# Layer 0's values: two halves of the array, or four quarters

## The reference, cut to what matters

```python
attn = jnp.einsum('bqhd,bkhd->hbqk', qh, kh)
attn = attn * mask[None]
attn = attn - jnp.max(attn)
attn = jnp.exp(attn) * mask[None]
attn = attn / (jnp.sum(attn, axis=-1, keepdims=True) + 1e-15)
out = jnp.einsum('hbqk,bkhd->bqhd', attn, vh).reshape(Bn, Tq, H * DK)
```

## Time and profile before

| | |
|---|---|
| three runs, median | 914.35 us |
| the profiled execution | 909.97 us |
| its span, first to last instruction | 908.2 us |
| PE busy | 861.4 us (95%), 4511 matmul records |
| DVE, ACT, POOL busy | 553.0, 416.2, 456.1 us |
| mean granted TensorE clock | 0.981 of full speed |
| L476, layer 0's values | 256 records, 62.0 us |
| L464, sums of both layers | 512 records, 68.2 us |
| first values step to the end of the loop | about 93 to 357 us |

### The profile page before, as it was taken

One profiled execution on the slowest core, in us unless ns is written; L12 is line 12 of the kernel. 1 busy time (PEld: TensorE's weight loads), 2 busy tenths in 40 slices (PEclk: granted clock), 3 DMA queues, 4 the chain that ended last, 5 costly groups with the idle time before them and its releaser, 6 DMA issues.

```text
span 908.2 us, 11986 instructions
## 1 busy us (share of the span) xinstructions
PE 861.4 (95%) x4511; PEld 577.5 (64%) x4511; DVE 553.0 (61%) x1050; ACT 416.2 (46%) x560; POOL 456.1 (50%) x284
## 2 busy tenths in 40 slices
PE   7989999999999989989989999999999999999865
PEld 6567475665747464467577587576775875767624
DVE  1347565656657575877575656655756566556646
ACT  2325363645545354633543644535536345353440
POOL 0520404124040424327689588687795886863714
PEclk9999999999999999998999999999999999999968
DMA  9613335161514225973531432424314334210011
GB/s 349 247 62 136 124 121 200 47 245 51 197 70 177 108 94 214 290 265 95 131 101 47 140 93 93 140 70 137 119 47 139 93 93 139 70 70 1 1 47 47
DMA packets 47641, 111.55 MB, mean 123 GB/s; under 512 B 4704, under 2 KB 8544, under 8 KB 47584
## 3 DMA queue, kind: packets, MB, share of 16 engines
q1 hardware_dynamic: 47584, 110.78, 36.4%
HBM read 76.69 MB, written 34.08 MB: 122 GB/s over the span
## 4 chain that ended last, share of the span: by engine, by line
PE 81%; DVE 11%; POOL 3%; issue 2%; DMA 2%; ACT 1%; SPq 0%; POOLq 0%; DVEq 0%
PE bank L416 18%; PE bank L417 17%; PE bank L418 16%; PE bank L464 6%; PE bank L476 6%; PE bank L457 5%; PE bank L586 3%; PE bank L626 3%; DVE den L1123 2%; PE bank L410 2%; PE bank L404 2%; POOL a_lo L1318 2%; DVE r_hi L1127 1%; DMA r_first<-r_dram 1%; DVE scores L1014 1%
## 5 line engine op out<-in xcount | busy, mean ns | idle before, releaser
L416 PE MATMUL bank<-wo_lo,a_hi 128*128 128x512 f32 x384 | 156.0, 406 | 7.9 <-POOL a_lo L1435 3.9
L1280 POOL TENSOR_TENSOR x_lo<-x_raw,x_hi 128x2048 fp32r<-128x2048 f32 x8 | 39.0, 4878 | 235.1 <-ACT x_hi L774 235.1
L417 PE MATMUL bank<-wo_hi,a_lo 128*128 128x512 f32 x384 | 151.0, 393 | 0.0
L418 PE MATMUL bank<-wo_hi,a_hi 128*128 128x512 f32 x384 | 150.8, 393 | 0.0
L990 DVE CUSTOM_DVE_ANT_0 scores<-bank,mask_f 128x512 f32<-128x512 f32 x128 | 80.8, 688 | 58.1 <-PE bank L457 58.1
L862 ACT ACTIVATE scores<-scores,sh 128x512 f32<-128x512 f32 x128 | 80.3, 711 | 59.0 <-DVE sh L1116 59.0
L1313 POOL TENSOR_TENSOR a_lo<-a_raw,a_hi 128x1024 fp32r<-128x1024 f32 x32 | 80.0, 2503 | 52.8 <-ACT a_hi L843 52.8
L416 PE MATMUL bank<-x_lo,wq_hi 128*128 128x512 f32 x256 | 102.2, 399 | 3.9 <-DVE q_lo L981 3.0
L417 PE MATMUL bank<-x_hi,wq_lo 128*128 128x512 f32 x256 | 99.9, 390 | 0.0
L418 PE MATMUL bank<-x_hi,wq_hi 128*128 128x512 f32 x256 | 99.7, 390 | 0.0
L784 ACT ACTIVATE q_hi<-bank,bq_sb 128x512 fp32r<-128x512 f32 x64 | 44.1, 690 | 114.7 <-PE bank L418 112.0
(11 more groups left out here) (134 smaller groups left out, 1563.5 us busy)
## 6 DMA issues: line engine op xcount, KB each, us to landing
u_dram<-u_out SPq DMA_DIRECT2D x8, 2048.0 KB, 7.4
a_raw<-u_dram SPq DMA_DIRECT2D x32, 512.0 KB, 3.6
r_bc<-r_dram SPq DMA_DIRECT2D x56, 256.0 KB, 5.0
x_raw<-x_t SPq DMA_DIRECT2D x8, 1024.0 KB, 5.6
xn<-x_n SPq DMA_DIRECT2D x8, 1024.0 KB, 5.5
xb_dram<-xn SPq DMA_DIRECT2D x8, 1024.0 KB, 5.2
z<-xb_dram SPq DMA_DIRECT2D x32, 256.0 KB, 2.8
out<-z SPq DMA_DIRECT2D x7, 1024.0 KB, 6.7
```

Of the source, the lines that this page charges most:

```text
L416: nc.tensor.matmul(dst, lh, rl, start=first, stop=False)
L417: nc.tensor.matmul(dst, ll, rh, start=False, stop=False)
L418: return nc.tensor.matmul(dst, lh, rh, start=False, stop=last)
```

## The change

Each head's 64 columns are computed as two matmuls of 32 columns instead of one of 64. `part` runs over G = 4 quarters of the chunk's 128 columns, and `part // 2` is the head within the chunk. Each result lands where it did before.

```diff
                 for c in range(2 * j, 2 * j + 2):
                     if not (i == 0 and c < 2):
                         pe.wait_ge(u_saved, (C0 + 1) * i + (c - 1 if c >= 2 else c - 2))
-                    for a in range(HC0):
-                        h = HC0 * c + a
-                        last = nc.tensor.matmul(U_BANKS[c % 2][a * DK0:(a + 1) * DK0, :],
-                                                v0[:, b, h * DK0:(h + 1) * DK0], scores[:, h, :],
+
+                    for part in range(G):
+                        h, first = HC0 * c + part // 2, c * P + 32 * part
+                        last = nc.tensor.matmul(U_BANKS[c % 2][32 * part:32 * part + 32, :],
+                                                v0[:, b, first:first + 32], scores[:, h, :],
                                                 start=True, stop=True)
                     last.then_inc(u_psum_ready, 1)
```

## The result

| | before | after |
|---|---|---|
| five runs, median | 914.13 us | 906.48 us |
| lowest to highest | 912.59 to 914.93 | 904.86 to 908.47 |
| profiled execution, span | 908.2 | 904.7 |
| PE busy, matmul records | 861.4 us, 4511 | 857.6 us, 4767 |

The ratio is 0.9922, 95% interval 0.9900 to 0.9944: 7.1 us faster, 5.1 to 9.1. 4.2 us and a time of 910.15 had been forecast, in a range of 908.2 to 912.5: right in sign and too small. The two profiled executions differ by only 3.5 us. So there are two questions: what the gain above 4.2 us is, and why this pair of profiles shows less than the times do.

What follows compares the result with a forecast made beforehand. PE's own instruction stream was taken to bound the loop. 28 steps at 0.15 us saved gave 4.2 us, all else 0, so the median 914.35 became 910.15 us, range 908.2 to 912.5.

Steps and rivals of the forecast that it cites:

- The bound: Loop, 93 to 357 us: PE's own stream sets the time, with one 3.0 us wait, for VectorE.
- The switch between values and sums: Each step: with quarters in both, the two passes of sums take 0.86 us for 1.00, 0.14 us less.
- the first filling: First values pass behind logits: shorter weight loads for 32 columns, 1.85 us for 1.87, 0.02 us less a step.
- Twice the instructions: Values in each step: 16 records where there were 8, and as many weight loads; cost taken as 0.
- two quarters that read one head: Values passes: two side-by-side streams read the same `scores` numbers; taken as 0, at worst a 0.43 us pass becomes 0.86.
- Rivals 1, 2 and 3: Gap not from shape (5%, 913.2 us); same-head quarters take turns (2%, up to 958 us); each record costs (3%, 921.4 us).
- The 3 us ahead of the last block: PE's 3.03 us idle before the loop's last block, from a VectorE and GpSimd collision, stays; range +0.9 to -1.
- The last block gains nothing: Four steps behind the loop: PE's 0.6 us gain becomes idle time waiting for GpSimd's `a_lo`; 0.
- the term for the landing of `r_first`: Behind the loop: stores and layer 1 weight loads start 0.5 us sooner beside `r_first`; its landing could suffer, at most +0.3.
- The saving lies in PE's stream and should be the same there: The profiled execution's 4.2 us saving was carried unchanged to the median of three runs: 914.35 to 910.15 us.
- Rival 4: Gain partly given back by a worse collision, later `r_first` and slower clock at the end: +1.5 to +2.5, about 912.2; 8%.
- The range's own terms: Around 910.15: step rounding 0.3, collision +0.9 and -1, DMAs 0.3, runs' spread about 1 us.

Runs made afterwards that it cites:

- Experiment 2: Kernel before with values half in halves, half in quarters per step: halves first, ratio 0.9998; quarters first, ratio 1.0050.
- experiment 4: Kernel before with quarters only in the last block, the four steps behind the loop; ratio 1.0007.
- experiment 3: Instructions added at PE's start: empty ones, before 0.9999, changed 0.9919; small matmuls moving the 16 KB packet, before 1.0009, changed 0.9965; all against before.

## Why the prediction was right about the loop and wrong behind it

- **The bound**, PE's own stream in the loop: right. The one wait stayed, and each step's gain went through in full.
- **The switch between values and sums, 0.14, and the first filling, 0.02:** right to 0.01 us. 28 steps gave 4.3 us, 4.2 forecast. Experiment 2 shows the cause of the 0.14 by moving and adding the switch; what the 0.02 is was not tested.
- **Twice the instructions, and two quarters that read one head: 0 each.** Right; the values piece is 1.85 us for 16 records, where 8 took 1.87. Rivals 1, 2 and 3 are out. The Trainium skill, "TensorEngine Tiling (Array Packing)", Instruction Overhead, states about 60 cycles of overhead for each matmul. The trace does not agree where the records run side by side: by these two pieces eight more cost nothing.
- **The 3 us ahead of the last block:** 3.03 us before and after, as forecast. What was not seen is that in part of the executions a fall of the clock adds to them: 8 of the 11 profiles that have the idle time show the lower level begin during it or within 1.3 us behind it. The profiles of before and after on which the sum and its check rest are two of the other three.
- **The last block gains nothing:** right for the block itself (experiment 4), with a wait of 0.30 us for ScalarE's copy where 0.1 had been estimated. But the term for the landing of `r_first` failed. The chain `den`, `r_dram`, `r_first` was worked out from the distances of the trace before, as if these hung on the loop's last logits alone, and the term was put at 0 to +0.3. The store to `r_dram` does keep its distance, 6.64 us; but `r_first` lands sooner, because the store of `u` ahead of it ends 1.5 us sooner: the longer program has its instruction packets elsewhere. The term is **-1.8 us** (the loop's 4.3 taken from 6.1 at equal clock, so with the same error of 0.4). Measured by itself, from the loop's end, VectorE's first `z` comes 1.8 us sooner in the first pair of profiles, and 2.1 sooner between the means of the first four profiles with the packet on the store and the first two without. The doubled instructions were weighed as time on PE, and not as bytes that a DMA has to bring.
- **"The saving lies in PE's stream and should be the same there":** the step from the profile to the median, and the second term that was put at nothing. Time at the lower clock is 37.7 us (+- 0.5) in 93 executions of before, and 35.1 (+- 1.2) in 17 of the changed kernel with and without empty instructions; 2.6 x 0.40 is **1.0 us** more of gain, with an error of 0.5. That this share is a consequence of the change, and not chance, isn't shown: groups of twelve executions whose loop is as long as before have 34.9 to 39.5 us of it. Rival 4, which had the same places give something back, named them rightly and had the sign wrong.
- **The sum:** 4.3 + 1.8 + 1.0 = 7.1, the measured difference. The 1.8 and the 1.0 are what is left over at each stage, so that the sum comes out says nothing by itself; the 1.8 stands on the profiles and on experiment 3.
- **Luck:** the profiled execution was a short one, one of ten in a hundred, and the median of 914.35 from three runs was 1.2 us above that of 93 executions, 913.17. This widens the distance between 910.15 and 906.48, but it isn't why the gain was 7.1 instead of 4.2. The range's own terms, added up, give 907.9 to 912.6, a little wider than the 908.2 to 912.5 stated; the measured time lies outside both.

## What to carry to other kernels

Where groups of small matmuls follow each other on TensorE, give them the same shape on the array even if that doubles their number: here every change between halves and quarters cost 0.13 to 0.15 us, and further matmuls side by side nothing. When a change adds or removes instructions, look in the trace at where the 16 KB instruction packets fall before and after; here one that fell on a transfer for which a chain waits cost about 2 us, and 52 or 64 instructions more moved it by 5 us. And a single profile of a kernel with stretches of slow clock is one draw: set its time beside several runs before adding to it.

## What the runs showed of the hardware

A 2 MB store took 6.4 to 6.5 us without a 16 KB instruction packet beside it and 7.7 to 8.3 with one. The packets beside it were 0.9 to 1.6 us long, and the store grew by 1.2 to 1.9 us, but not in proportion: the shortest packet, 0.88 us, went with 8.2 us and the longest, 1.57, with 8.0. 64 empty instructions on PE did not move the packets; 16 small f32 matmuls, 32 matmul and 32 weight-load records, did by some 5 us.

A product of VectorE that takes 2.28 us was held for 3.8 us by an addition on GpSimd, while GpSimd's was 2.1 us longer than its 4.6. The rows fit each waiting for the other to end: GpSimd's began 0.07 us behind VectorE's product at 326.84, which ended at 329.12, and ended itself at 333.60, 4.5 us later; VectorE's next product ended 2.14 us after that the earlier trace rows. PE's list of waits shows only the 3.0 us under `q_lo`, and neither the product nor the addition that caused them.
